# End of the first cross attention: batch tails, router rows and first expert tiles in another order

## The chip, the cores and the metric

The kernel runs on one core of one Trainium2 chip. The metric is the time of one execution on the device in microseconds, as the median of several runs.

## The reference

The input is `x` of 32 batches x 128 tokens x 128 channels, with a context of 32 x 77 x 128. Four blocks follow one another, each added to its input:

```python
x = x + cross_attention_0(context, layernorm(x))   # 16 heads of 64 for q, 4 for k and v, rmsnorm of q and k
x = x + experts(layernorm(x))                      # router over 8 experts, the best 2 of each token
x = x + cross_attention_1(layernorm(x), context)   # 16 heads of 8
x = x + ffn(...)                                   # 2 layers of local attention and a gated feed forward
```

The two blocks that matter here are the first attention and the experts:

```python
attn = softmax(q @ k.T); out = (attn @ v).reshape(B, S_q, H * D) @ wo.T
router_logits = layernorm(x) @ wg.T                 # the two largest of 8, their softmax shares
y = (silu(x @ w1[e].T) * (x @ w3[e].T)) @ w2[e].T    # for the experts e chosen by the token
```

## The kernel before

One program per engine is written out by hand, and the engines meet at semaphores only: TensorE (PE), VectorE (DVE), ScalarE (ACT), GpSimd (POOL) and the DMA queue of SyncE (SP). Each engine executes its own list strictly in the order written.

**First attention.** It is a software pipeline over the 32 batches. In step i the body works on batch i-1 (projections), on i-2 (scores, exponentials), on i-3 (the probabilities `a_p` are turned by 16 transposes, L547, in two halves; ACT, L667, and DVE, L870, copy the halves to `a_pT`; then come the products with the values, L591, and their copy to `a_oT`, L686), on i-4 (output projection, L623, and the addition to `X`, L924, with mean and variance, L933 to L988, and the root on POOL, L993), and on i-5 (a router row: normed by DVE, L718, transposed, L497, copied, L841, multiplied by the gate, L503, and the two largest of 8 found, L848 and L851). After every fourth router row the group of four gets its places in the experts' regions, and POOL scatters the rows to HBM with indirect DMAs (L1009). The router's transpose and the output projection write the same 128 columns of the PSUM tile `R[0]`, so the one has to wait until the other has been read.

**Experts.** The work is 80 tiles of up to 128 routed rows, 40 for each half of the batches (`SEG` = 2). Step i of the tiles transposes the input of tile i (L1102, after which ACT and DVE split it into a high and a low part, L1152 and L1175), does the three products of tile i-1 with w1 and w3 (L459 to L461), the two transposes of tile i-2 (L1125) and the products of tile i-3 with w2 (L1137). ACT makes the silu of tile i-1 (L1157), which needs another table of functions than the exponentials. DVE multiplies with it (L1183) and copies the result (L1190). The tiles of the first half need the rows of the first 16 batches only, so their inputs wait in SBUF long before the attention ends. The tiles of the second half need the rows of all batches.

**Where the two meet.** The attention's pipeline is unrolled up to its step 34, and then the first `HEAD` = 16 steps of the tiles are written out, with what is left of the attention put between them. Conditions on i do that on each engine, on PE for instance:

```python
            for i in range(HEAD):
                step(SEG * NT, 8, tiles, i)
                if i == 0:
                    step(NB, 8, body, NB + 3)
                if i == 2:
                    router(It(NB + 4, (NB + 4) % 8, NB, 8, 1))
```

Step 34 of the attention does, on PE, the transposes of batch 31, the router row of batch 29, the values of batch 31 and the output projection of batch 30. Between tile steps 0 and 1 stands step 35 with the router row of batch 30 and the output projection of batch 31. The router row of batch 31 follows between tile steps 2 and 5. The places of the last group (`group_placed`), the count per expert (`totals`), the tables of the second half (`tables`, `tables_rest`), the positions (`answers`) and the shares of the two experts come between later tile steps.

## Time and profile before

| | us |
|---|---|
| median of 3 runs | 1665.03 |
| lowest and highest of them | 1663.01, 1668.54 |
| the profiled execution | 1662.99 |
| its span | 1661.2 |

| engine | busy, us | share of the span |
|---|---|---|
| PE | 1483.0 | 89% |
| DVE | 1257.8 | 76% |
| ACT | 1112.5 | 67% |
| POOL | 892.5 | 54% |

The profiled execution took 1662.99 us, of which 1661.2 lie between its first and its last instruction. Times below are counted from the start of this span. The granted clock of PE is given as a share of its full 2.4 GHz, so that 0.50 is the lower level of 1.2 GHz. A product in f32 can show as two matmuls, which is why 8 products of the program are x16 in some rows. Matmuls are pipelined, so the end of one and the start of the next overlap.

### The profile page before, as it was taken

The page shows a single profiled execution, that of the slowest core. Times are in us where ns is not written, and L with a number is a line of the kernel's source. Part 1 is how long each engine was busy: PE and PEld are TensorE (multiplying, and loading weights), DVE is VectorE, ACT ScalarE, POOL GpSimd, SP SyncE. Part 2 cuts the span into 40 slices and gives each one's busy share as a digit, 9 for nine tenths or more (in the row PEclk, how much of TensorE's full clock was granted, in tenths as well). Part 3 has the DMA queues.
Part 4 walks back from the last instruction along what each step waited for, and adds up shares of the span by engine and source line. Part 5 has one row for each costly group of instructions (what it writes and reads, how often), then busy time and mean ns, then how long its engine had stood idle before and what let it go on. Part 6 is the DMA issues. An engine that isn't in the chain of part 4 may idle for free.

```text
span 1661.2 us, 38597 instructions
## 1 busy us (share of the span) xinstructions
PE 1483.0 (89%) x12380; PEld 1229.9 (74%) x12443; DVE 1257.8 (76%) x3064; ACT 1112.5 (67%) x2630; POOL 892.5 (54%) x789
## 2 busy tenths in 40 slices
PE   4888888888878998999986999999888999999888
PEld 3777777677766886777765888888776788888766
DVE  6888888888846557898874788888565677777766
ACT  4877777677735556888773777777532777777632
POOL 5667777677723104555424677777402777777600
PEclk9999999999979998999997999999899999999999
DMA  9700000000012322100000000000000000000000
GB/s 384 304 1 9 9 10 11 8 17 11 10 33 82 87 76 65 36 18 20 16 9 7 15 14 15 13 15 14 8 9 4 9 16 13 15 13 15 9 18 38
DMA packets 75554, 61.30 MB, mean 37 GB/s; under 512 B 40256, under 2 KB 61120, under 8 KB 74688
## 3 DMA queue, kind: packets, MB, share of 16 engines
q1 hardware_dynamic: 71360, 51.69, 9.6%
q0 software_dynamic: 4096, 8.40, 1.7%
q8 instruction: 50, 0.82, 0.2%
q14 instruction: 48, 0.39, 0.1%
HBM read 21.30 MB, written 30.41 MB: 31 GB/s over the span
## 4 chain that ended last, share of the span: by engine, by line
DVE 43%; PE 25%; ACT 18%; issue 9%; POOL 3%; DVEq 1%; DMA 1%; SPq 0%; ACTq 0%; POOLq 0%
ACT d_p L708 10%; DVE slot L1713 5%; DVE d_ss L1696 5%; DVE d_B L1704 4%; DVE d_A L1702 4%; PE slot L459 4%; ACT d_sq L1633 4%; PE slot L460 3%; PE slot L461 3%; PE slot L1832 3%; PE slot L547 3%; DVE c_nm L1377 2%; PE slot L1137 2%; DVE a_mx L728 2%; PE slot L623 2%
## 5 line engine op out<-in xcount | busy, mean ns | idle before, releaser
L1750 POOL TENSOR_TENSOR d_r<-d_vv,nhalf 128x16 f32<-128x16 f32 x64 | 186.1, 2907 | 210.6 <-DVE d_vv L1701 210.6
L993 POOL TENSOR_TENSOR rs<-mv,nhalf 128x1 f32 (+1 forms) x160 | 97.9, 612 | 255.0 <-DVE mv L988 190.1
L708 ACT ACTIVATE d_p<-slot,d_nm,d_r 128x128 f32<-128x128 f32 x512 | 185.6, 468 | 49.3 <-DVE d_nm L1717 49.3
L708 ACT ACTIVATE a_p<-slot,a_nm,a_rq 128x77 f32<-128x77 f32 x512 | 163.8, 429 | 36.0 <-DVE a_nm L732 36.0
L1696 DVE TENSOR_REDUCE d_ss<-d_sq 128x16 f32<-128x1024 f32 x64 | 78.1, 1220 | 99.0 <-ACT d_sq L1633 99.0
L1752 POOL TENSOR_TENSOR d_A<-d_A,d_B 128x1024 f32<-128x1024 f32 x64 | 151.3, 2364 | 0.0
L708 ACT ACTIVATE c_p<-slot,c_nm 128x77 f32<-128x77 f32 x512 | 117.4, 361 | 8.6 <-DVE c_nm L1377 8.3
L1617 PE MATMUL slot<-d_v,d_pT 128*128 128x65 f32 x1024 | 121.4, 272 | 0.0
L1617 PEld LDWEIGHTS slot<-d_v,d_pT 128*128 128x128 f32 x1024 | 119.6, 192 | 0.0
L1347 ACT ACTIVATE c_pT<-slot 77x1024 f32<-77x1024 f32 x64 | 67.0, 1047 | 40.5 <-PE slot L1271 40.4
L1048 POOL TENSOR_TENSOR a_rq<-a_vvq,nhalf 128x16 f32<-128x16 f32 x32 | 93.4, 2918 | 0.0
L1713 DVE TENSOR_REDUCE slot<-slot 128x8 f32<-128x1024 f32 x64 | 78.9, 1232 | 12.6 <-PE slot L1590 9.5
L1633 ACT ACTIVATE d_sq<-slot 128x1024 f32<-128x1024 f32 x64 | 67.8, 1059 | 24.8 <-PE slot L461 24.8
L1475 POOL DMA_INDIRECT c_yg<-answers,c_gi x64 | 64.0, 1001 | 36.7 <-POOL c_gi L1471 26.3
L1590 PEld LDWEIGHTS slot<-d_qT 64*128 64x128 f32 x1024 | 62.7, 189 | 27.5 <-issue 27.5
L1704 DVE TENSOR_TENSOR d_B<-slot,T 128x512 f32<-128x512 f32 x128 | 81.8, 681 | 0.0
L1860 ACT ACTIVATE f_gl<-slot,b1l 128x512 f32<-128x512 f32 (+1 forms) x48 | 32.8, 684 | 72.6 <-PE slot L461 72.6
L1271 PE MATMUL slot<-ident,c_p 128*77 128x128 f32 x512 | 71.0, 284 | 11.2 <-ACT c_pT L1347 10.5
L1637 ACT ACTIVATE d_qT<-slot 128x1024 f32<-128x1024 f32 x64 | 65.7, 1027 | 20.3 <-PE slot L1563 20.3
L1009 POOL DMA_INDIRECT routed<-r_xn,r_ps x64 | 64.8, 1013 | 25.0 <-issue 15.9
L1611 PE MATMUL slot<-wol,d_oT 128*128 128x128 f32 x512 | 74.0, 288 | 4.6 <-ACT d_oT L1650 4.6
L1702 DVE TENSOR_TENSOR d_A<-slot,T 128x1024 f32<-128x1024 f32 x64 | 77.9, 1218 | 0.0
(283 smaller groups left out, 4546.2 us busy)
## 6 DMA issues: line engine op xcount, KB each, us to landing
routed<-zero SPq DMA_DIRECT2D x2, 9216.0 KB, 48.9
b_x<-routed SPq DMA_DIRECT2D x80, 64.0 KB, 1.8
answers<-b_y SPq DMA_DIRECT2D x40, 128.0 KB, 1.9
X<-in_x SPq DMA_DIRECT2D x2, 1024.0 KB, 7.3
d_zx<-Z SPq DMA_DIRECT2D x64, 32.0 KB
H<-Z SPq DMA_DIRECT2D x64, 32.0 KB
out<-f_o SPq DMA_DIRECT2D x8, 256.0 KB, 2.0
d_zx<-Z SPq DMA_DIRECT2D x64, 31.8 KB
```

Source lines behind the costliest of these rows:

```text
L708: i = e.activation(t["p"][:, h, :], R[slot][:, k // nbank, nk * (k % nbank):nk * (k % nbank) + nk], ACT.Exp, bias=t["nm"][:, h:h + 1], sca ...
L993: return e.tensor_tensor(rs[:, bass.ds(b, 1)], mv[:, bass.ds(b, 1), 1:2].rearrange("p a b -> p (a b)"), nhalf[:, 0:1], ALU.pow)
L1048: e.tensor_tensor(a["rq"][:, it.m(1, 2), :], a["vvq"][:], nhalf[:, 0:16], ALU.pow).then_inc(S("a_rq"), 1)
L1611: mm = e.matmul(R[1][:, 0, 0:128], t["oT"][:, c, :], wol[:, l, c, :], start=(c == 0), stop=(c == 3))
L1617: mm = e.matmul(R[3][:, h // 4, 65 * (h % 4):65 * (h % 4) + 65], t["pT"][:, 4 * (h % 2) + h // 2, :], t["v1"][:, it.m(4, 4), h, :], start= ...
L1633: e.activation(t["sq"][:].rearrange("p (a b) -> p a b", a=2), qk_slot(it)[:], ACT.Square).then_inc(S("d_sq"), 1)
L1696: e.tensor_reduce(t["ss"][:, p, :], t["sq"][:].rearrange("p (h d) -> p h d", d=DL), AX.X, ALU.add)\
L1702: e.tensor_tensor(A, qk, T1[:, l, :, :].unsqueeze(2).to_broadcast([128, 2, HL, DL]), ALU.mult)
L1704: i = e.tensor_tensor(Bt[:, :, :, 32 * h:32 * h + 32], qk[:, :, :, 32 - 32 * h:64 - 32 * h], T2[:, l, :, 32 * h:32 * h + 32].unsqueeze(2). ...
L1713: e.tensor_reduce(R[0][:, 0, 0:8], R[2][:].rearrange("p a (j k) -> p a j k", k=128), AX.X, ALU.max, negate=True)\
L1750: e.tensor_tensor(t["r"][:, p, :], t["vv"][:, p, :], nhalf[:, 0:16], ALU.pow).then_inc(S("d_key"), 1)
L1752: e.tensor_tensor(t["A"][:, p, :], t["A"][:, p, :], t["B"][:, p, :], ALU.add).then_inc(S("d_key"), 1)
```

## The change

The work and the data are the same. The order on PE, ACT and DVE at the end of the attention is another, and one small activation is added. The pieces of the body become functions (`turned`, `values`, `output`, `second_half`, `added`, `measured`), the common pipeline ends one step earlier (`last_step=NB + 2`), and step 34 is written out piece by piece:

- PE: tile step 0 goes first, then the first half of the transposes of batch 31, the output projection of batch 30, the second half, and the values of batch 31. The output projection of batch 31 follows tile step 1, which holds the first products of tile 0. `output(..., False)` leaves out the wait for a router row, since none stands ahead of it any more.
- The router rows of batches 29, 30 and 31 come after tile steps 2 and 3, 4 and 5, 6 and 7. Places and count move back by two steps (PE 7 to 9 and 9 to 11, DVE 8 to 10), the tables from 10 and 11 to 12 and 13, the positions from 12 and 13 to 14 and 15, the shares behind the last step, and the exponential of the shares on ACT from step 9 to 10.
- ACT: a silu of two elements is put ahead of the wait for the values of batch 31, so that the silu's table is loaded there.

```diff
+            def turned(it, half):
+                b, slot = it.b(3), (2, 3)[half]
+                if half == 0:
...
+                e.wait_ge(S(("ac_na", "ac_nb")[half]), count(b))
+                for c in range(8):
+                    h = 8 * half + 4 * (c // 4) + 2 * (c % 2) + c // 2 % 2
+                    mm = e.transpose(R[slot][0:SK, c // 4, 128 * (c % 4):128 * (c % 4) + 128], a["p"][:, h, :], ident[:])
+                mm.then_inc(S(("ac_PTa", "ac_PTb")[half]), 1)
+
+            def values(it):
+                b = it.b(3)
...
+            def output(it, routed=True):
+                b = it.b(4)
...
+                    if routed and it.b(5) is not None:
+                        e.wait_ge(S("r_v"), count(it.b(5), 4, 4))
+                    if routed and it.b(6) is not None and it.m(6, GB) == 3:
+                        e.wait_ge(S("r_ps"), count(it.b(6)))
+                    e.wait_ge(S("ac_oTe"), count(b))
+                    for c in range(8):
+                        mm = e.matmul(R[0][:, 0, 0:128], a["oT"][:, it.m(4, 2), c, :], wo0[:, c, :], start=(c == 0), stop=(c == 7))
+                    mm.then_inc(S("ac_wo"), 1)
...
-            pipeline(e, NB, 8, 8, body, [A_PART], totals, last_step=NB + 3)
+            pipeline(e, NB, 8, 8, body, [A_PART], totals, last_step=NB + 2)
 
             tiles = b_tensor(e)
-            for i in range(HEAD):
+            tail = [It(NB + i, (NB + i) % 8, NB, 8, 1) for i in range(6)]
+            step(SEG * NT, 8, tiles, 0)
+            turned(tail[2], 0)
+            output(tail[2], False)
+            turned(tail[2], 1)
+            values(tail[2])
+            for i in range(1, HEAD):
                 step(SEG * NT, 8, tiles, i)
-                if i == 0:
-                    step(NB, 8, body, NB + 3)
-                if i == 2:
-                    router(It(NB + 4, (NB + 4) % 8, NB, 8, 1))
-                if i == 4:
-                    logits(It(NB + 4, (NB + 4) % 8, NB, 8, 1))
-                if i == 7:
-                    router(It(NB + 5, (NB + 5) % 8, NB, 8, 1))
+                if i == 1:
+                    output(tail[3], False)
+                if i in (2, 4, 6):
+                    e.wait_ge(S("ac_add"), NB)
+                    if i > 2:
+                        e.wait_ge(S("r_v"), count(NB - 5 + i // 2, 4, 4))
+                    router(tail[1 + i // 2])
+                if i in (3, 5, 7):
+                    logits(tail[1 + i // 2])
                 if i == 9:
+                    router(tail[5])
+                if i == 11:
                     totals(1)
             e.wait_ge(S("r_nr"), SEG)
             return tiles
...
                     e.wait_ge(S("a_nma"), count(b))
                     exponentials(e, a, 2, 0, 4, SK, S("ac_expa"), a["rq"][:, it.m(2, 2), :])
+                if it.static and it.i == NB + 2:
+                    e.activation(g_["s"][:, 0, 0:2], eps[:, 0, :], ACT.Silu)
...
-            pipeline(e, NB, 8, 4, body, [A_PART], last_step=NB + 3)
+            pipeline(e, NB, 8, 4, body, [A_PART], last_step=NB + 2)
 
             tiles = b_scalar(e)
-            for i in range(HEAD):
+            step(SEG * NT, 4, tiles, 0)
+            step(NB, 4, body, NB + 2)
+            for i in range(1, HEAD):
                 step(SEG * NT, 4, tiles, i)
-                if i == 9:
+                if i == 10:
                     e.wait_ge(S("r_dl"), NB)
                     e.activation(r_["dn"][:], r_["dl"][:], ACT.Exp).then_inc(S("r_ex"), 1)
             return tiles
...
+            def added(it):
+                b = it.b(4)
+                if b is not None:
+                    e.wait_ge(S("ac_wo"), count(b))
+                    e.tensor_tensor(rows(X, b), rows(X, b), R[0][:, 0:1, 0:128], ALU.add).then_inc(S("ac_add"), 1)
...
-            pipeline(e, NB, 16, 8, body, [A_PART], both_tables, last_step=NB + 3)
+            pipeline(e, NB, 16, 8, body, [A_PART], both_tables, last_step=NB + 2)
 
             tiles = b_vector(e)
-            for i in range(HEAD):
+            tail = [It(NB + i, (NB + i) % 8, NB, 8, 1) for i in range(6)]
+            step(SEG * NT, 4, tiles, 0)
+            added(tail[2])
+            second_half(tail[2])
+            measured(tail[2])
+            row_normed(tail[2])
+            for i in range(1, HEAD):
                 step(SEG * NT, 4, tiles, i)
-                if i == 0:
-                    step(NB, 8, body, NB + 3)
                 if i == 1:
-                    row_normed(It(NB + 4, (NB + 4) % 8, NB, 8, 1))
-                if i == 3:
-                    row_turned(It(NB + 4, (NB + 4) % 8, NB, 8, 1))
-                if i == 5:
-                    row_chosen(It(NB + 4, (NB + 4) % 8, NB, 8, 1))
-                if i == 6:
-                    group_chosen(It(NB + 4, (NB + 4) % 8, NB, 8, 1))
-                if i == 8:
-                    group_placed(It(NB + 5, (NB + 5) % 8, NB, 8, 1))
+                    added(tail[3])
+                    measured(tail[3])
+                if i in (2, 4, 6):
+                    row_turned(tail[1 + i // 2])
+                if i in (3, 5, 7):
+                    row_chosen(tail[1 + i // 2])
+                    if i < 7:
+                        row_normed(tail[2 + i // 2])
+                if i == 7:
+                    group_chosen(tail[4])
                 if i == 10:
+                    group_placed(tail[5])
+                if i == 12:
                     tables(1)
-                if i == 11:
+                if i == 13:
                     tables_rest(1)
-                if 12 <= i < 12 + SEG:
-                    answers(i - 12)
-                if i == 14:
-                    shares()
+                if i >= 14:
+                    answers(i - 14)
+            shares()
             return tiles
```

The order of PE from the last transposes of the attention to the first products of tile 0 (`wo_127` is the output weight wo0, `a_p` the probabilities, `r_xn` a router row, `b_x` a tile's input, `w13h` the expert weights). Before:

```order
L547 MATMUL slot<-ident,a_p 77x128 x16
L497 MATMUL slot<-ident,r_xn 128x128
L503 MATMUL slot<-wg,r_xT 128x8
L591 MATMUL slot<-a_pT,a_vt 64x256 x8
L623 MATMUL slot<-wo_127,a_oT 128x128 x8
L1102 MATMUL slot<-ident,b_x 128x128
L497 MATMUL slot<-ident,r_xn 128x128
L503 MATMUL slot<-wg,r_xT 128x8
L623 MATMUL slot<-wo_127,a_oT 128x128 x8
L1102 MATMUL slot<-ident,b_x 128x128
L1107 TENSOR_LOAD t_expert
L459 ISA
```

The same stretch of PE in the changed kernel:

```order
L1141 MATMUL slot<-ident,b_x 128x128
L516 MATMUL slot<-ident,a_p 77x128 x8
L554 MATMUL slot<-wo_127,a_oT 128x128 x8
L516 MATMUL slot<-ident,a_p 77x128 x8
L534 MATMUL slot<-a_pT,a_vt 64x256 x8
L1141 MATMUL slot<-ident,b_x 128x128
L1146 TENSOR_LOAD t_expert
L459 ISA
L459 MATMUL slot<-w13h,b_xTl 128x512
L460 REGISTER_ALU
L460 MATMUL slot<-w13l,b_xTh 128x512
L461 MATMUL slot<-w13h,b_xTh 128x512
```

Two router rows (L497, L503) have gone from the stretch, one output projection stands between the two halves of the transposes, and the other one follows the products of tile 0.

On DVE, between tile steps 2 and 5, the changed kernel has this (`r_xT`, `r_mx`, `r_ix` and `r_xn` belong to router rows, the `b_` names to tiles):

```order
L864 COPY r_xT<-slot 128x128
L1214 TENSOR_TENSOR b_xTl<-slot,b_xTh 128x128
L1222 TENSOR_TENSOR b_g<-slot,b_s 128x256
L1229 COPY b_y<-slot 128x128
L871 MAX r_mx<-slot 128x8
L874 MAX_INDEX r_ix<-r_mx,slot 128x8
L741 TENSOR_SCALAR r_xn<-X,mv,rs 128x128
L1214 TENSOR_TENSOR b_xTl<-slot,b_xTh 128x128
L1222 TENSOR_TENSOR b_g<-slot,b_s 128x256
L1229 COPY b_y<-slot 128x128
L864 COPY r_xT<-slot 128x128
```

Before, only the row of batch 31 was spread over the tiles. Now the four small operations of a row come three times, once in every two steps.

## Rows read from the trace of the kernel before

**Rows 1.** The profile page, its first line.

```profile
span 1661.2 us, 38597 instructions
```

**Rows 2.** Waits from 462 to 487 us: total, times, longest.

```profile
ACT a_oT L686 <- PE slot L591: 8.5, 1, 8.5
```

**Rows 3.** Stretches: length; busy PE, PEld, DVE, ACT, POOL (instructions); clock; DMA; GB/s.

```profile
462.00:466.00 4.00, 1.54 (x13) 1.15 (x11) 2.41 (x7) 3.04 (x8) 1.21 (x1) 1.00 0.00 0
466.00:477.00 11.00, 8.90 (x41) 6.37 (x42) 2.64 (x9) 1.02 (x1) 2.63 (x3) 0.53 0.03 12
...
480.00:487.00 7.00, 5.47 (x22) 5.05 (x23) 1.24 (x7) 0.41 (x2) 1.71 (x2) 0.51 0.05 19
487.00:505.00 18.00, 17.19 (x107) 12.91 (x106) 10.12 (x45) 12.24 (x31) 6.43 (x8) 1.00 0.27 79
505.00:518.00 13.00, 9.02 (x49) 6.63 (x49) 12.12 (x43) 5.15 (x18) 11.47 (x10) 1.00 0.29 88
...
530.00:620.00 90.00, 88.03 (x551) 72.41 (x550) 49.05 (x164) 51.69 (x165) 4.26 (x6) 1.00 0.29 82
```

**Rows 4.** Order of time, PE: start, us, engine, line, operation, [idle before <-releaser].

```profile
458.55 1.95 PE L591 MATMUL slot<-a_pT,a_vt 77*64 77x256 f32 x16
460.43 2.05 PE L623 MATMUL slot<-wo,a_oT 128*128 128x128 f32 x16
463.71 1.07 PE L547 MATMUL slot<-ident,a_p 128*77 128x128 f32 x8 [1.24 <-POOL a_p L715]
466.06 1.57 PE L547 MATMUL slot<-ident,a_p 128*77 128x128 f32 x8 [1.28 <-DVE a_p L715]
470.65 3.68 PE L591 MATMUL slot<-a_pT,a_vt 77*64 77x256 f32 x16
474.26 3.21 PE L623 MATMUL slot<-wo,a_oT 128*128 128x128 f32 x16
482.57 3.75 PE L623 MATMUL slot<-wo,a_oT 128*128 128x128 f32 x16 [0.96 <-DVE r_ix L851]
487.87 0.33 PE L1102 MATMUL slot<-ident,b_x 128*128 128x128 f32 x1 [0.39 <-DVE b_xTl L1175]
488.17 0.49 PE L459 MATMUL slot<-w13h,b_xTl 128*128 x1
488.73 0.40 PE L461 MATMUL slot<-w13h,b_xTh 128*128 x1
```

**Rows 5.** Order of time, DVE and ACT, at the end of the attention.

```profile
465.12 0.80 DVE L715 TENSOR_TENSOR a_p<-a_p,a_rc 128x616 f32<-128x616 f32 x1
467.67 1.22 DVE L870 COPY a_pT<-slot 77x1024 f32<-77x1024 f32 x1 [1.02 <-PE slot L547]
474.38 1.02 ACT L686 ACTIVATE a_oT<-slot 128x1024 f32<-128x1024 f32 x1 [8.54 <-PE slot L591]
486.87 1.28 ACT L1157 ACT_TABLE_LOAD   x1
488.16 0.39 ACT L1157 ACTIVATE b_s<-slot 128x256 f32<-128x256 f32 x1
```

**Rows 6.** Order of time, the router row of batch 31 between the tiles.

```profile
488.92 0.34 DVE L718 TENSOR_SCALAR r_xn<-X,mv,rs 128x128 f32<-128x128 f32 x1
489.40 0.30 PE L497 MATMUL slot<-ident,r_xn 128*128 128x128 f32 x1
491.89 0.28 DVE L841 COPY r_xT<-slot 128x128 f32<-128x128 f32 x1
492.81 0.29 PE L503 MATMUL slot<-wg,r_xT 128*128 128x8 f32 x2
495.47 0.16 DVE L848 MAX8 r_mx<-slot 128x8 f32<-128x8 f32 x1
495.86 0.17 DVE L851 FIND_INDEX8 r_ix<-r_mx,slot 128x8 uint32<-128x8 f32 x1
```

**Rows 7.** Order of time, PE: the input of tile 12, behind the tables.

```profile
508.17 0.33 PE L1102 MATMUL slot<-ident,b_x 128*128 128x128 f32 x1 [1.36 <-DVE b_xTl L1175]
```

More of the change, by code:

```diff
@@ new lines, in values @@
+            def values(it):
+                b = it.b(3)
+                if b is not None:
+                    if it.seen(1):
+                        e.wait_ge(S("ac_v"), it.upto(1))
+                    if it.static:
+                        if it.seen(2):
+                            e.wait_ge(S("a_qTe"), it.upto(2))
+                        if it.seen(4):
+                            e.wait_ge(S("ac_oTe"), it.upto(4))
+                    e.wait_ge(S("ac_pTa"), count(b))
+                    e.wait_ge(S("ac_pTb"), count(b))
+                    for g in range(HK0):
+                        for odd in range(2):
+                            mm = e.matmul(R[1][64 * odd:64 * odd + 64, g // 2, 256 * (g % 2):256 * (g % 2) + 256],
+                                          a["v"][0:SK, it.m(3, 4), DH0 * g:DH0 * g + DH0],
+                                          a["pT"][0:SK, 4 * g + 2 * odd:4 * g + 2 * odd + 2, :].rearrange("p a b -> p (a b)"),
+                                          start=True, stop=True)
+                    mm.then_inc(S("ac_PV"), 1)
@@ L536, in body @@
                 if b is not None:
-                    for half, slot in ((0, 2), (1, 3)):
-                        if half == 0:
-                            if it.seen(3):
-                                e.wait_ge(S("ac_expa"), it.upto(3))
-                        else:
-                            if it.seen(3):
-                                e.wait_ge(S("ac_expb"), it.upto(3))
-                        e.wait_ge(S(("ac_na", "ac_nb")[half]), count(b))
-                        for c in range(8):
-                            h = 8 * half + 4 * (c // 4) + 2 * (c % 2) + c // 2 % 2
-                            mm = e.transpose(R[slot][0:SK, c // 4, 128 * (c % 4):128 * (c % 4) + 128], a["p"][:, h, :], ident[:])
-                        mm.then_inc(S(("ac_PTa", "ac_PTb")[half]), 1)
+                    for half in range(2):
+                        turned(it, half)
                 b = it.b(1)
@@ L609, in body @@
                     mm.then_inc(S("a_pj"), 1)
-                b = it.b(4)
-                if b is not None:
-                    if it.seen(1):
-                        e.wait_ge(S("a_ev"), nth(it.upto(1), 3, 3))
-                    if it.static:
-                        if it.seen(5):
-                            e.wait_ge(S("ac_add"), it.upto(5))
-                    if it.b(5) is not None:
-                        e.wait_ge(S("r_v"), count(it.b(5), 4, 4))
-                    if it.b(6) is not None and it.m(6, GB) == 3:
-                        e.wait_ge(S("r_ps"), count(it.b(6)))
-                    e.wait_ge(S("ac_oTe"), count(b))
-                    for c in range(8):
-                        mm = e.matmul(R[0][:, 0, 0:128], a["oT"][:, it.m(4, 2), c, :], wo0[:, c, :], start=(c == 0), stop=(c == 7))
-                    mm.then_inc(S("ac_wo"), 1)
+                output(it)
                 if it.static and it.i == 3:
@@ L871, in body, with measured @@
                         .then_inc(S("ac_pTb"), 1)
+            def added(it):
+                b = it.b(4)
+                if b is not None:
+                    e.wait_ge(S("ac_wo"), count(b))
+                    e.tensor_tensor(rows(X, b), rows(X, b), R[0][:, 0:1, 0:128], ALU.add).then_inc(S("ac_add"), 1)
+            def measured(it):
+                b = it.b(4)
+                if b is not None:
+                    e.wait_ge(S("ac_add"), count(b))
+                    apart(e)
+                    e.bn_stats(st[:, 0, :], rows(X, b)).then_inc(S("ac_bn"), 1)
+                    stats_tail(e, b, S("ac_bn"), S("ac_ag"), S("ac_ve"))
+            def body(it):
+                b = it.b(0)
+                if b is not None:
+                    layernorm(e, X, a["xn"], b, it.m(0, 2)).then_inc(S("ac_xn"), 1)
+                second_half(it)
                 row_normed(it)
@@ L920, in body @@
                     i.then_inc(S("a_kTe"), 1)
[L921 to L924 removed]
+                added(it)
                 b = it.b(2)
@@ L929, in body @@
                     normalize(e, a, slice(8, 16), SK).then_inc(S("ac_nb"), 1)
[L930 to L934 removed]
+                measured(it)
                 if it.static and it.i < NB // ST:
```

44 lines of the change are left out of this document (13 added, 31 removed).

## The prediction

> **What bounds the kernel now.** The page comes first: the span is 1661.2 us [rows 1], and the profiled execution took 1662.99. The change touches only the seam between the first attention and the expert tiles, so the second view is the waits from 462 to 487 us. The longest stands at ACT: 8.5 us in one piece until PE has made the values of batch 31 [rows 2]. The third view is the stretches. The reader is to see that no engine is full in the seam. From 462 to 466 us PE is busy for 1.54 of 4 us, and from 466 to 477 DVE is busy for 2.64, ACT for 1.02 and POOL for 2.63 of 11 us; PE shows 8.90, but at a granted clock of 0.53 [rows 3]. The batches left are one chain of transposes, copies, values, projection, addition, root and router row, and PE executes it in written order. From 487 us on the tiles fill PE, 17.19 of 18 us and later 88.03 of 90 at clock 1.00 [rows 3]. So the seam is a latency, and behind it a stage starts in which PE sets the pace. Whatever brings the first tiles forward brings all 80 tiles and what follows forward by as much, unless something else is late then.
>
> The last view is the order of time. It fixes two marks. The program is unchanged up to the output projection of batch 29, which ends at 460.43 + 2.05 = 462.48. The second mark is the transpose of tile 2's input, at 487.87 [rows 4]. In both programs it stands behind the last output projection and the first products of tile 0. Between the marks lie 25.39 us.
>
> **The change part by part.** I walk the new order of PE between these marks, with durations at full clock where a row has one.
>
> 1. Tile 0's transpose, about 0.3, falls into the gap ahead of the transposes of batch 31. These start at 463.71, because POOL's normalization releases them [rows 4], and nothing of that moves: to 463.71.
> 2. The first half of the transposes is 1.07 [rows 4]: 464.78.
> 3. The output projection of batch 30, 2.05 as at 460.43 [rows 4]: 466.83. Its input was copied a step earlier, and its wait for the router is dropped. It delays the second half of the transposes, which is ready when DVE's normalization ends, 465.12 + 0.80 = 465.92 [rows 5], by 0.9.
> 4. The second half, 1.07 like the first: 467.90.
> 5. DVE copies it, 1.22 [rows 5], plus 0.05 for the handover: 469.17. The addition of batch 30 stands ahead on DVE and is over by about 467.2.
> 6. The values of batch 31, 1.95 as those of batch 30 at 458.55 [rows 4]: 471.12. The router row of batch 29 no longer stands here.
> 7. ACT's copy, 1.02 [rows 5], plus 0.05: 472.19. Tile 1's transpose lies beside it.
> 8. The products of tile 0. They write a bank that this copy reads, so they start behind it. From 488.17 to the last one's start at 488.73 and on to its issue's end are some 0.8 us [rows 4]: 472.99.
> 9. The output projection of batch 31, 2.05: 475.04. Then tile 2's transpose, at about 475.1.
>
> That is 487.87 - 475.1 = **12.8 us** sooner, if PE's clock is full.
>
> **Clock.** The rows show 1.00 up to 466 us, then 0.53 until 477 and 0.51 from 480 to 487 [rows 3]. It fell after a stretch in which PE was busy for 1.54 of 4 us. In the new order the same stretch holds about 3 of 4 us, and the gaps that are left are some 0.9, 1.3 and 1.0 us. So it may stay up, but the values and projections come in bursts. At the lower level (1.2 GHz) the values took 3.68 in place of 1.95, and a projection 3.21 or 3.75 in place of 2.05 [rows 4], 1.2 to 1.7 more for each such burst. The bounds are none of them and three, 0 to 4.9. I take one, **-1.5**, since the new seam is fuller than the one in which the clock fell, and less full than the tiles.
>
> The Trainium skill says on the page "TensorE: Matmul & The Clock Gate", section "What's actually happening", that the throttled state is the default and that activity releases it. The trace agrees in that the clock came back while the projection of batch 31 ran.
>
> **Router rows.** Two more rows, of batches 29 and 30, now stand between tiles on a full PE. Each has a transpose of 0.30 and a gate product of 0.29 [rows 6], which makes 2 x 0.59 = **-1.2**. On DVE a row costs 0.34 for the norm, 0.28 for the copy, and from 495.47 to 496.03 for the largest two [rows 6], 1.2 in all. From 487 to 505 DVE was busy for 10.12 of 18 us [rows 3], so two rows more, 2.4 us, fit into the free time of some eight tiles. I cost them at nothing, with up to 1.5 if DVE comes late with a tile's low part.
>
> **Silu's table.** Its load, 1.28, now lies in ACT's wait for the values, where 8.5 us were free and some 5 remain. Before, it stood ahead of the first silu, which started right behind it at 488.16 [rows 5]. PE was on tile 1's products until 488.73 + 0.23 and lost little by it. I take 0, and 0.6 as the upper bound.
>
> On the page "ScalarE: Activation LUTs", section "What ACT_TABLE_LOAD costs", the Trainium skill puts a switch at 1283 ns of load and 1380 ns of drain. The load of 1.28 agrees and no such drain is seen ahead of 488.16; with it the sum would be some 1.4 us better.
>
> **Late things.** Places, tables and positions are the same work with the same stall: tile 12's input waited 1.36 for DVE behind the tables [rows 7], and PE was busy for 9.02 of 13 us there [rows 3]. They move back by two tile steps, that is some 3.5 us, against 10 gained, so they too come earlier in time. The inputs of the second half's tiles need them from tile 40 on. That is 24 tiles behind the written-out ones. The 551 matmuls in 90 us [rows 3], at 10 for a tile, make 1.64 us for each, 39 us together, so neither SP's loads nor POOL's scatters delay it. POOL's three instructions of 2.63 us from 466 to 477 [rows 3] are a root and the two scatters that stand between the roots of batches 30 and 31. They fit between the two additions, which by the steps above lie 8 us apart.
>
> **Sum.** 12.8 - 1.5 - 1.2 = **10.1 us** gained. Against the profiled execution's own time that is 1662.99 - 10.1 = 1652.9. The median of the runs is 2.0 higher, at 1665.03, and would give 1654.9. The lowest run equals the profiled one. I put the forecast in the middle, at **1654.0**, from a base of 1664.0.
>
> **The rivals.**
>
> *Lost between the tiles.* A router row now passes from PE to DVE and back in every two steps, and POOL or DVE may be late with it: PE's transpose of a row waits for the previous row's largest two, for the norm and for the last addition. If each of the six pieces stopped PE for about 1 us, less than the 1.36 of [rows 7], 6 of the 10 us would go, and the time would be 1660, no change that can be told. Against it: between 487 and 505 us PE was busy for 17.19 of 18 us although one such row passed through there [rows 3]. Chance 0.08.
>
> *The change does less than it says.* The second half of the transposes waits for the projection of batch 30. If the three bursts of the clock's upper bound ran at the lower level, the gain would be 12.8 - 4.9 - 1.2 = 6.7 and the time 1657.3. That is inside the forecast's range.
>
> *Slower: the clock through the tiles.* The rows of the router cut the tiles' stream on PE, and if PE is granted the lower level through the 14 written-out steps that follow, each tile of 1.64 us takes about 1.3 longer, by the ratio of 3.75 to 2.05 of the projection [rows 4]. This is 18 us against 10, and the time is 1672. It decides if the clock falls again behind 476 us and doesn't come back before the places are made; two tiles at that level would not be enough. Against it: from 505 to 518 us PE was busy for only 9.02 of 13 and kept 1.00 [rows 3]. Chance 0.04.
>
> **How the numbers follow.** The forecast with its clock variants has 0.88. A measurement of this kernel can tell about 0.3%, or 5.0 us, from no change. The gain's own bounds are 12.8 + 0.6 - 0 = 13.4 and, with three bursts at the lower level, DVE's 1.5 and the rows' 1.2, 12.8 - 4.9 - 1.5 - 1.2 = 5.2. From 1664.0 that gives 1650.6 to 1658.8. The runs shown spread by 5.5 us, so I put one us on the lower and half a one on the upper end: 1649.5 to 1659.3. The rivals on the far side, at 1660 and 1672, stay out, with 0.12. Faster by over 0.3% is 0.88, within it 0.08, slower by over 0.3% 0.04.
>
> **What the new profile would show.** Tile 0's first products should start near 472, not 486, and tile 2's transpose near 475 to 477. ACT's wait for the values should shrink from 8.5 to 4 or 5 us with a table load inside it. The clock between 466 and 480 should be well above 0.53. The tiles should fill PE from about 476 on, with no idle time over 0.5 us at L497 or L503, and the shift of 10 us should still be there at tile 40 and at the last tile. I am wrong if the shift is there at tile 2 and has gone by the last tile, or if the second half of the transposes or the copy behind it waits for something that I have not named.

## The result, and the profile after

| | before | after |
|---|---|---|
| median of the runs of the comparison, us | 1666.09 (20 runs) | 1659.62 (20 runs) |
| lowest, highest | 1661.67, 1681.12 | 1652.89, 1668.67 |
| profiled execution, its span | 1662.99, 1661.2 | 1662.73, 1660.9 |

The ratio is 0.9961, 95% interval 0.9947 to 0.9976: 6.5 us or 0.39% faster, where 10.1 us were forecast. The profiled executions differ by 0.26 us only, because the part behind the tiles took 1046.1 us in that of after and 1040.3 in that of before (more on this part below). The page shows about the same busy times as before:

```profile
span 1660.9 us, 38661 instructions
...
PE 1488.3 (90%) x12442; PEld 1232.7 (74%) x12443; DVE 1258.8 (76%) x3064; ACT 1112.3 (67%) x2631; POOL 892.2 (54%) x789
```

Waits of the changed kernel from 462 to 487 us (total, times, longest), to be read against [rows 2]:

```profile
ACT a_oT L707 <- PE slot L534: 3.5, 1, 3.5
```

The 8.5 us of ACT have become 3.5. The stretches of the changed kernel (columns as in [rows 3]):

```profile
462.00:466.00 4.00, 2.87 (x27) 2.66 (x26) 2.44 (x6) 3.35 (x10) 1.21 (x1) 1.00 0.06 16
466.00:477.00 11.00, 8.68 (x51) 7.33 (x50) 3.79 (x12) 2.84 (x5) 5.15 (x6) 0.72 0.09 31
480.00:487.00 7.00, 6.41 (x44) 5.37 (x44) 4.91 (x22) 3.57 (x12) 3.13 (x4) 1.00 0.33 97
487.00:505.00 18.00, 14.03 (x92) 10.61 (x90) 11.70 (x52) 9.81 (x26) 6.35 (x7) 1.00 0.28 82
505.00:518.00 13.00, 9.52 (x50) 7.78 (x51) 9.25 (x27) 4.57 (x15) 7.42 (x6) 0.87 0.17 51
530.00:620.00 90.00, 86.32 (x540) 71.02 (x540) 50.21 (x171) 50.46 (x161) 4.97 (x8) 1.00 0.27 78
```

From 480 to 487 us PE is now at full clock on tiles, where it stood at 0.51 before [rows 3]. Two stretches fall short. From 466 to 477 the clock is 0.72, better than 0.53 but not full. And from 505 to 518, where the positions and the shares now stand together, it is 0.87, where it was 1.00. The seam in order of time, PE and one row of ACT, against [rows 4, 5]:

```profile
464.55 1.95 PE L554 MATMUL slot<-wo,a_oT 128*128 128x128 f32 x16
465.78 1.28 ACT L703 ACT_TABLE_LOAD   x1
468.77 1.95 PE L534 MATMUL slot<-a_pT,a_vt 77*64 77x256 f32 x16 [1.41 <-DVE a_pT L890]
471.93 0.79 PE L459 MATMUL slot<-w13h,b_xTl 128*128 x1 [0.92 <-ACT a_oT L707]
473.37 3.62 PE L554 MATMUL slot<-wo,a_oT 128*128 128x128 f32 x16
476.77 0.42 PE L1141 MATMUL slot<-ident,b_x 128*128 128x128 f32 x1
```

The projection of batch 30 and the values take 1.95, full clock. Behind the pause of 0.92 the first product takes 0.79, where [rows 4] has 0.49, and the last projection 3.62: one burst at the lower level. Tile 2 is turned at 476.77, where it was 487.87. That is 11.1 us sooner. The shift is 10.3 at tile 17 (519.22 before, 508.93 after). At tile 18 it is 6.0 (521.01, 514.98), and it stays at 6.1 up to tile 79 (620.89, 614.78). So more than four us go in a single step, between tiles 17 and 18. All engines there, in the changed kernel:

```profile
506.71 2.25 POOL L1490 MEMSET c_vz<- 128x2560 f32 x1
508.11 0.42 DVE L836 TENSOR_TENSOR h_eq<-h_eq,h_dx 128x256 f32<-128x256 f32 x1
508.56 0.42 DVE L839 TENSOR_REDUCE h_sh<-h_eq 128x32 f32<-128x256 f32 x1
508.88 1.84 POOL L1491 MEMSET d_v<- 128x2080 f32 x1
508.93 0.27 PE L1141 MATMUL slot<-ident,b_x 128*128 128x128 f32 x1
509.13 1.86 DVE L982 TENSOR_SCALAR r_w<-r_dn 128x32 f32<-128x32 f32 x1
511.02 0.35 DVE L984 RECIPROCAL r_w<-r_w 128x32 f32<-128x32 f32 x1
511.41 0.19 DVE L986 TENSOR_TENSOR r_w<-r_dn,r_w 128x32 f32<-128x32 f32 x1
511.82 0.29 DVE L1214 TENSOR_TENSOR b_xTl<-slot,b_xTh 128x128 fp32r<-128x128 f32 x1 [0.21 <-DVE r_w L986]
512.26 0.79 PE L459 MATMUL slot<-w13h,b_xTl 128*128 x1 [3.06 <-DVE b_xTl L1214]
514.98 0.39 PE L1141 MATMUL slot<-ident,b_x 128*128 128x128 f32 x1
```

DVE does the last positions (to L841, not all shown) and the three operations of the shares (L982 to L986) in one go. The first share operation, 128 x 32 elements, shows 1.86 us, and ends 0.27 after POOL's memset of `d_v` (508.88 + 1.84 = 510.72, and 509.13 + 1.86 = 510.99). The low part of the next tile comes behind all that. PE waits 3.06 us for it, and resumes at the lower clock. In the kernel before, the same operation met only the memset's last part:

```profile
514.58 1.85 POOL L1452 MEMSET d_v<- 128x2080 f32 x1
516.07 0.61 DVE L949 TENSOR_SCALAR r_w<-r_dn 128x32 f32<-128x32 f32 x1
```

### The profile page after: what moved, and what is told of

It is laid out like the page before. It is cut to its first block, busy times and chain, and to the rows that moved or that the text cites. A ratio compares the mean times of both kernels' runs of the same rounds, so it can differ in the third digit from the quotient of the medians.

```text
span 1660.9 us, 38661 instructions
## 1 busy us (share of the span) xinstructions
PE 1488.3 (90%) x12442; PEld 1232.7 (74%) x12443; DVE 1258.8 (76%) x3064; ACT 1112.3 (67%) x2631; POOL 892.2 (54%) x789
## 4 chain that ended last, share of the span: by engine, by line
DVE 43%; PE 25%; ACT 18%; issue 9%; POOL 3%; DVEq 1%; DMA 1%; SPq 0%; ACTq 0%; POOLq 0%
ACT d_p L731 10%; DVE slot L1752 5%; DVE d_ss L1735 5%; DVE d_B L1743 4%; DVE d_A L1741 4%; PE slot L459 4%; ACT d_sq L1672 4%; PE slot L460 3%; PE slot L461 3%; PE slot L1871 3%; PE slot L516 3%; DVE c_nm L1416 2%; PE slot L1176 2%; DVE a_mx L751 2%; DVE c_rcT L1469 1%
## 5 line engine op out<-in xcount | busy, mean ns | idle before, releaser
L613 PE MATMUL slot<-a_kb,a_qT 128*128 128x154 f32 x512 | 77.5, 294 | 0.7 <-ACT a_pT L686 0.4
```

The source lines that it names most:

```text
L613: mm = e.matmul(R[slot][:, k // 2, 2 * SK * (k % 2):2 * SK * (k % 2) + 2 * SK], a["qT"][:, c, :], a["kb"][:, it.m(2, 2), c // 2, :], start ...
```

## The experiments

Theories at the start: (A) the memset on POOL holds the share operation; (B) the lump of positions and shares on DVE is too long by itself; (C) the clock fall in the seam is the loss. The early silu was a fourth suspect.

**How the runs are read.** The runs come in three groups, each on a chip of its own; the tables number them. Medians did not separate the variants: the 95% intervals of the ratios are 0.3% to 0.7% wide, 5 to 11 us. Behind the tiles, from tile 79's transpose to the end of the span, executions took 1040 to 1052 us in the first pair and on the chips of groups 2 and 3, without an order by kernel, and 1071 to 1080 in group 1, whose chip is slower. So the traces are compared up to tile 79, from a mark before anything changed: the start of the addition of batch 29 on DVE. The table gives the start of a tile's transpose (L1102 or L1141) less this mark, and the duration of the one DVE operation in dispute. The run b_before is the kernel before unchanged, c_after and c_after_again are the changed kernel unchanged. Each row is one trace.

| group, kernel | tile 2 | 10 | 17 | 18 | 20 | 40 | 79 | first share |
|---|---|---|---|---|---|---|---|---|
| before | 25.36 | 39.35 | 56.71 | 58.50 | 61.47 | 94.44 | 158.38 | 0.61 |
| after | 14.33 | 30.15 | 46.49 | 52.54 | 55.59 | 88.41 | 152.34 | 1.86 |
| 1 c_after | 14.44 | 31.52 | 56.18 | 58.24 | 61.18 | 94.06 | 157.98 | 0.17 |
| 1 e1 | 12.10 | 29.11 | 50.49 | 52.81 | 55.76 | 88.59 | 152.51 | 0.17 |
| 1 e2 | 12.12 | 29.20 | 52.77 | 55.00 | 57.95 | 90.82 | 154.82 | 0.17 |
| 1 e3 | 12.12 | 29.20 | 52.81 | 55.98 | 58.92 | 91.76 | 155.72 | 0.17 |
| 2 b_before | 23.94 | 37.85 | 55.21 | 57.00 | 59.97 | 92.91 | 156.88 | 0.62 |
| 2 b8 | 23.94 | 37.81 | 54.87 | 56.87 | 59.84 | 92.77 | 156.69 | 0.17 |
| 2 e7 | 12.06 | 27.89 | 44.78 | 46.97 | 49.92 | 82.75 | 146.74 | 0.17 |
| 2 e4 | 12.07 | 27.75 | 44.10 | 50.11 | 53.43 | 86.33 | 150.37 | 1.86 |
| 3 c_after_again | 12.07 | 27.87 | 44.65 | 49.84 | 53.59 | 86.46 | 150.40 | 1.47 |
| 3 e1_again | 12.07 | 27.88 | 44.62 | 47.70 | 50.65 | 83.49 | 147.42 | 0.17 |
| 3 e2_again | 12.07 | 27.84 | 44.15 | 46.35 | 49.30 | 82.12 | 146.05 | 0.17 |
| 3 e9_all | 12.07 | 27.64 | 43.97 | 46.16 | 49.26 | 82.16 | 146.04 | 0.17 |

| run | median, us | the kernel before beside it | ratio, 95% interval |
|---|---|---|---|
| c_after | 1699.13 | 1702.19 | 0.9968 [0.9950, 0.9987] |
| e1 | 1693.96 | same | 0.9958 [0.9941, 0.9975] |
| e2 | 1696.12 | same | 0.9968 [0.9950, 0.9986] |
| e3 | 1696.12 | same | 0.9962 [0.9948, 0.9976] |
| b_before (1 execution) | 1673.58 | 1671.06 | none |
| b8 | 1668.47 | same | 0.9991 [0.9962, 1.0021] |
| e7 | 1654.87 | same | 0.9914 [0.9881, 0.9947] |
| e4 | 1656.82 | same | 0.9908 [0.9880, 0.9935] |
| c_after_again | 1657.72 | 1668.23 | 0.9925 [0.9895, 0.9955] |
| e1_again | 1655.88 | same | 0.9928 [0.9903, 0.9953] |
| e2_again | 1657.96 | same | 0.9932 [0.9905, 0.9958] |
| e9_all | 1656.43 | same | 0.9912 [0.9884, 0.9940] |

**The changed kernel again, group 1.**

> The changed kernel once more, as it is, to see whether what its first trace shows repeats. Two theories. A (a stall at the seam's end): the first trace has a shift of 10.3 us against the kernel before up to tile 17's input, and 6.0 from tile 18 on to tile 79, since DVE makes the positions of the second half and the shares in one piece, and the shares' first operation takes 1.86 us beside a memset of POOL. A expects the shift again at 10.3 at tile 17 and at 6 from tile 18 on, DVE's first share operation at 1.8 to 1.9 us, PE idle for about 3 us ahead of the next products, and a time 6 us below that of the kernel before (ratio 0.996). B (given back later, at random): the 6 us of the times come out of the later stages, so the shift at tile 79 may be 10 in this trace.

The signs that A named did not repeat: the first share took 0.17 and the stall between tiles 17 and 18 was gone (2.06 us). B is not decided, since group 1 has no trace of the kernel before and so shows no shift. Yet nothing was gained by the missing stall, as another operation was held, for longer:

```profile
507.43 0.95 POOL L1048 DMA_INDIRECT routed<-r_xn,r_ps  x1 [0.30 <-issue]
507.69 4.96 DVE L822 TENSOR_SCALAR t_read<-h_ba 128x40 int32<-128x40 f32 x1
508.37 2.26 POOL L1490 MEMSET c_vz<- 128x2560 f32 x1
510.55 1.86 POOL L1491 MEMSET d_v<- 128x2080 f32 x1
512.72 0.17 DVE L825 SCALAR_TENSOR_TENSOR h_dx<-h_dx,region 128x8 f32<-128x8 f32 x1
```

A conversion of 128 x 40 elements, 0.18 us in the first trace, lasts until 512.65, 0.24 behind the end of both memsets (512.41). The memsets meet whatever DVE happens to be at, here the tables.

**e1: the memsets behind the shares.**

```diff
             e.wait_ge(S("ac_add"), count(NB - 1))
+            e.wait_ge(S("r_w"), 11)
             e.memset(c_["vz"][:], 0.0).then_inc(S("c_const"), 1)
```

> POOL's four memsets wait for the shares, so that nothing of POOL runs beside them. If the memset holds the first share operation up (A1), it falls from 1.86 to 0.2 to 0.6 us, the idle time of PE ahead of the products of tile 16 from 3.1 to about 1.8, and the shift at tile 79 grows from 6 to 7.3 or more, up to 8.5 if PE's clock no longer falls there. If the operation is slow by itself or the size of the lump on DVE is all that counts (A2), nothing changes: 1.86 and a shift of 6.

Neither operation is held. The conversion stands in the same place as in c_after, some 0.27 after the start of POOL's last indirect DMA (505.16 here), and only the memset behind that DMA is gone:

```profile
505.43 0.18 DVE L822 TENSOR_SCALAR t_read<-h_ba 128x40 int32<-128x40 f32 x1
...
513.23 2.23 POOL L1491 MEMSET c_vz<- 128x2560 f32 x1 [7.10 <-DVE r_w L986]
```

Tile 79 is 5.5 us sooner than in c_after (152.51 against 157.98), of which 2.3 are already there at tile 2: c_after had the seam's clock fall and e1 had not. That leaves 3.1 for the memsets on this chip. The median is 5.2 lower, and doesn't decide by itself. With nothing held, e1 still isn't free of a stall: from tile 2 to tile 17 it takes 38.39 us, where the same program takes 32.55 in e1_again, and its clock from 505 to 518 is 0.74 (0.65 in c_after). This loss belongs to group 1 and isn't explained (see the slower chip, at the end).

**e2: the shares in time for step 11**, with a semaphore `r_sh` of their own.

```diff
+                if i == 11:
+                    shares()
...
-            shares()
...
-            e.wait_ge(S("r_w"), 11)
+            e.wait_ge(S("r_sh"), 3)
```

> The shares are made behind tile step 11, away from the positions and from the memsets. If the lump of positions and shares together with the memset costs the 4.3 us (A), PE's wait of 3 us ahead of tile 16's products is gone or under 1 us, the shift at tile 79 is 9 to 10, and the time is 9 to 10 us below that of the kernel before, ratio 0.994. If only the memset counts, it is 7.5 to 8.5. If the change's gain is lost in later stages (B), the time does not move against the changed kernel whatever the shift.

The first share took 0.17, but the memset held the tables, 4.97:

```profile
504.56 4.97 DVE L822 TENSOR_SCALAR t_read<-h_ba 128x40 int32<-128x40 f32 x1
505.25 2.25 POOL L1491 MEMSET c_vz<- 128x2560 f32 x1
```

So moving the shares alone protects the shares alone.

**e3: no early silu.** The activation of two elements is left out; it has no part in the result.

```diff
-                if it.static and it.i == NB + 2:
-                    e.activation(g_["s"][:, 0, 0:2], eps[:, 0, :], ACT.Silu)
```

> The silu of two elements is left out, so that the table is loaded ahead of the first real silu. The first forecast put its worth at 0, 0.6 at most: PE is on the output projection of batch 31 for over 2 us (3.6 in the first trace) while ACT loads for 1.28 us, so the shift at tile 2 and the time stay within 0.3 us and 0.1%. If a switch costs 2.7 us with a drain, as the Trainium skill has it on the page ScalarE: Activation LUTs, it is still below 3.6, but the first silu would start 2.7 instead of 1.3 us behind the end of tile 0's products.

```profile
472.77 1.28 ACT L1194 ACT_TABLE_LOAD   x1
474.06 0.38 ACT L1194 ACTIVATE b_s<-slot 128x256 f32<-128x256 f32 x1
```

Tile 2 stands at 12.12, as with the silu (12.10 and 12.12). Tile 79 stands 2.3 ahead of c_after, which is c_after's clock fall. The early table is worth nothing that a trace shows.

**The kernel before, and it with late memsets.** b8 has e1's wait in the program before.

> The kernel before once more, for a trace from the same chip as the runs beside it. In the runs so far an operation of DVE on data in SBUF took far longer than its work where POOL's memsets ran (1.86 in place of 0.17 us for the first share, 4.96 in place of 0.18 for the row addresses of the second half's tiles, L822). If that is a matter of where the two meet in time, this kernel shows which of its operations meet a memset here: the theory A1 expects that any such operation of one input that starts within the memsets' 6 us ends only when they do, and that those outside take 0.2 us.

> The kernel before with POOL's four memsets behind the shares. A1 (memsets hold DVE up): tables and shares take 0.2 us each per operation, and the time falls by the stall that b_before's trace shows, 0.5 to 5 us. It is also the fair partner of the changed kernel with late memsets: if the change in order itself is worth 10 us as forecast, that kernel stays some 8 to 10 us below this one (ratio 0.994 to 0.995). If the order is worth only what the times showed, 5 to 6 us, the distance is that.

The first share goes from 0.62 to 0.17, tile 79 from 156.88 to 156.69, and the ratio has 1 inside. The kernel before had nothing to lose there:

```profile
513.68 1.85 POOL L1452 MEMSET d_v<- 128x2080 f32 x1
515.17 0.62 DVE L949 TENSOR_SCALAR r_w<-r_dn 128x32 f32<-128x32 f32 x1
```

The expected 0.5 to 5 us did not come. The held operation is thus a cost that came with the change of order. The theory in the expectation of b_before was also too wide: TENSOR_REDUCE, which has one input too, started inside the memset of `c_vz` at 511.56 and again inside that of `d_v` at 513.88, and took 0.42 both times, as it does alone.

**e7: both.** e2, and the memsets behind the positions (`r_w` at 8).

> The changed kernel with both: the memsets wait for the positions, and the shares are made behind tile step 11. A1 alone expects what late memsets alone gave, 10.3 to 11 us at tile 17 and at tile 79 against the kernel before on this chip with no memset in the way. A2 (the lump of positions and shares costs time of its own) expects 1 to 1.5 us more than late memsets alone.

```profile
507.51 0.19 DVE L841 SCALAR_TENSOR_TENSOR r_pos<-h_sh,r_pr 128x32 uint32<-128x32 f32 x1
507.83 2.23 POOL L1492 MEMSET c_vz<- 128x2560 f32 x1 [3.27 <-DVE r_pos L841]
508.14 0.49 PE L459 MATMUL slot<-w13h,b_xTl 128*128 x1 [0.45 <-DVE b_xTl L1215]
```

PE waits 0.45 at the place where it waited 3.06, and its product takes 0.49. Tile 17 to 18 is 2.2 us. Tile 79 is 10.1 us ahead of b_before: the shift survives. That is just short of the 10.3 to 11 expected. In this trace the clock was at its lower level from 497 to 501 us, between tiles 13 and 14, which goes with a tile 17 that is 0.6 to 0.8 later than in e9_all and e2_again (below).

**e4: PE kept busy in the seam.** Transposes of the identity, whose results nobody reads, stand in the two pauses.

```diff
+            def busy(slot, n):
+                for c in range(n):
+                    e.transpose(R[slot][:, 0, 128 * (c % 4):128 * (c % 4) + 128], ident[:], ident[:])
...
             turned(tail[2], 1)
+            busy(1, 10)
             values(tail[2])
+            busy(2, 7)
```

> Ten transposes of the identity into a free bank while PE waits for the second copy of the probabilities, and seven while it waits for the copy of the values' products; nobody reads them. In two of five traces of the changed order the projection of batch 31 took 3.62 us at the lower clock, in the other three 1.95. If PE's idle gaps bring the clock down there, it is 1.95 now and the clock 1.00 from 462 to 480 us, worth 2.2 us in those executions and about 1 us in the median. If the fall has another cause, it stays, and the extra products may add up to 0.5 us where they end later than the copy they bridge. The stall behind the tables stays as it is.

Tile 2 stands at 12.07, like the unfilled kernels without a fall. They are at full clock as well: e7, in the same group and not filled, has 12.06. So the fill costs nothing, and since the clock fell in only 2 of the 9 unfilled traces of this seam (after and c_after), two filled ones without a fall prove nothing. The run is inconclusive on the fill. On the other point it is clear: with the seam at full clock, tile 17 to 18 still takes 6.0 us and the first share 1.86. (C) is not the main loss.

**Group 3, one chip: the changed kernel, e1, e2 and everything.** e9_all is e7 with e4's fill.

> The changed kernel as partner of the three beside it, since the chips differ. By the traces so far the tiles lose 3.6 to 4.3 us between the inputs of tiles 17 and 18 (6.0 us in place of 1.8 to 2.2) if the first share starts inside a memset, as in the first trace; if the row addresses start inside one, as in c_after, they lose more and the share nothing. One of the two is expected, and 1 to 3 us in the seam by PE's clock.

> Memsets behind the shares, on another chip. Seen from the addition of batch 29, tile 79's input comes at 146.7 us with late memsets and early shares and at 150.4 to 152.3 with the stall. A1 (the memset alone): r_w takes 0.17 us, PE does not wait 3 us, its clock stays up, and tile 79 is at 147 to 147.5. A2 (the lump of positions and shares counts for itself): 148 to 149, with a wait of PE of 1.3 to 2 us ahead of the products of tile 16.

> Shares behind tile step 11, memsets where they were. If no row address meets a memset (they start about 0.7 us later than in the changed kernel, and the memsets came 1.5 to 2.4 us behind them in two traces), tile 79 is at 146.7 to 147.5 as with both changes; if one does, as on the slower chip, it stops for up to 5 us and tile 79 is at 151 or later. Either way the first share takes 0.2 us.

> Late memsets, early shares and the filled gaps together. PE's clock stays at 1.00 through the seam in every execution and no operation of DVE meets a memset: tile 2's input at 12.1, tile 79's at 146.7, and a median 1 us below that of late memsets with early shares, since the seam's clock fell in some executions only; 9 to 11 us below the kernel before by the trace, with a ratio of 0.991 to 0.994.

The four seams are equal at tile 2 (12.07). The share beside the memset, and then PE, in c_after_again:

```profile
507.87 1.84 POOL L1491 MEMSET d_v<- 128x2080 f32 x1
508.51 1.47 DVE L982 TENSOR_SCALAR r_w<-r_dn 128x32 f32<-128x32 f32 x1
511.25 0.49 PE L459 MATMUL slot<-w13h,b_xTl 128*128 x1 [2.67 <-DVE b_xTl L1214]
```

and in e1_again:

```profile
505.31 0.17 DVE L982 TENSOR_SCALAR r_w<-r_dn 128x32 f32<-128x32 f32 x1
506.22 2.23 POOL L1491 MEMSET c_vz<- 128x2560 f32 x1 [3.74 <-DVE r_w L986]
506.75 0.49 PE L459 MATMUL slot<-w13h,b_xTl 128*128 x1 [1.36 <-DVE b_xTl L1214]
```

The same stretch of 20 us (columns as in [rows 3]) in c_after_again:

```profile
500.00:520.00 20.00, 15.34 (x81) 12.48 (x80) 14.66 (x47) 7.81 (x24) 10.51 (x9) 0.88 0.24 70
```

in e1_again:

```profile
500.00:520.00 20.00, 16.84 (x104) 13.43 (x102) 13.36 (x49) 9.64 (x32) 7.91 (x6) 1.00 0.26 76
```

and in e2_again:

```profile
500.00:520.00 20.00, 17.52 (x104) 14.02 (x105) 14.28 (x52) 9.67 (x31) 9.89 (x8) 1.00 0.30 86
```

The clock goes from 0.88 to 1.00 and PE executes 104 matmuls in place of 81. Tile 79 stands at 150.40, then 147.42 with late memsets, then 146.05 with early shares. The memset cost 3.0 us (A): 2.1 of it lie between tiles 17 and 18 (5.19 against 3.08), and 0.8 between tiles 18 and 20, where the clock had fallen behind PE's wait (3.75 against 2.95).

Tile 79 of e1_again is where A1 put it (147 to 147.5), with the wait that A2 named. Of the 1.4 between e1_again and e2_again the lump (B) explains 0.9: tile 17 to 18 takes 3.08 with it and 2.20 without, and the wait of 1.36 left in e1_again is 0.45 in e7. The other 0.5 is there at tile 17 already. It goes with a fall of the clock around tile 13, in e1_again:

```profile
492.00:502.00 10.00, 7.98 (x33) 5.85 (x34) 7.30 (x28) 4.84 (x13) 7.26 (x8) 0.83 0.30 91
```

and in e2_again no such fall:

```profile
492.00:502.00 10.00, 7.91 (x45) 5.64 (x44) 7.54 (x31) 6.49 (x17) 5.47 (x6) 1.00 0.30 89
```

c_after_again and e7 had it too (0.83 in the same stretch), after, e4 and e9_all had not (1.00), so it goes neither with the shares nor with the memsets. The 3.0 of A is free of it, as both traces had it; the 0.9 of B rests on one pair. In group 1 the lump doesn't show: e1 takes 2.32 from tile 17 to 18 and e2 2.23, but e1 at the lower clock.

e2_again kept its memsets early and had nothing held in this trace, but on the chip of group 1 the same program lost 4.97 in the tables. e9_all gets 146.04 with the memsets out of the way as well.

The medians of these four runs lie within 2.1 us of each other and their intervals overlap, so a version that beats the change is not shown by the times. By the traces e7 (of group 2), e2_again and e9_all reach tile 79 some 3.7 to 4.4 us sooner than c_after_again. The ratios don't follow: the lowest, 0.9908, is that of e4, which still has the stall.

## Why the prediction was right in part

**The bottleneck and the seam: right.** Tile 2's transpose was forecast near 475.1 at full clock, 476.6 with one slow burst; it came at 476.77 with one slow burst. The projection of batch 30 was to start at 464.78 (464.55), the values at 469.17 (468.77), ACT's copy to end at 472.19 (the products followed at 471.93). The gain at full clock, 12.8 by the steps, is 25.36 - 12.07 = 13.3 against the first trace of before and 23.94 - 12.07 = 11.9 against b_before, whose own clock fell later.

**The clock: right for one execution, no property of the kernel.** "One burst, -1.5" was 2.3 where it occurred (14.33 - 12.07), since the products of tile 0 run slowly too. But 7 of 9 traces of this seam have no fall. One reading of the old rows was wrong: the clock had not come back while the projection of batch 31 ran. That one was slow to its end (3.75, to 486.32, clock 0.50 from 485.0 to 486.3). It came back during the projection of batch 30, which the 3.21 at 474.26 shows. And the bound of 4.9 for three slow bursts isn't the sum of its rows, 1.73 + 1.16 + 1.70 = 4.6. Neither changes the forecast.

**Router rows: right.** Forecast 1.2. From tile 2 to 79 the kernels with nothing held and no lump need 133.98 (e2_again), 133.97 (e9_all) and 134.68 (e7, with the clock's fall at tile 13), against 133.02 and 132.94 before: 1.0, and 1.7 with the fall. The rival that lost six single microseconds on these rows didn't occur, though its time, 1660, is what was measured. No idle time over 0.5 us stands at the router's two lines in the trace of after. It stands at the tiles' own operands, where the tables now come: 0.74, 0.78 and 1.02 ahead of three of them from 498 to 505 us, the stall that the forecast called the same.

**Silu's table: right at 0,** by e3.

**The step that failed** is the one on late things: "Places, tables and positions are the same work with the same stall". The work is the same; its neighbours are not. The sum has nothing for it, and it took 4.3 us. The prediction judged it by one deadline only, the inputs of tile 40, and DVE's extra operations by the free time of a whole stretch. Two things were missed. The shares, moved behind the last written step, now follow the positions of the second half directly, and DVE serves the tiles only when both are done. And POOL's memsets, which it hadn't listed, follow its last scatters and came 5.7 us forward with them (the one of `d_v` from 514.58 to 508.88), while the first share came 6.9 forward (516.07 to 509.13) and so met 1.2 us more of it. Both lie between tiles 17 and 18, 6.05 us in place of 1.79. The sum, mended, in the first pair of traces: seam 11.0, tiles 2 to 17 -0.8 (32.16 against 31.35), tile 17 to 18 -4.3, the rest +0.1, together 6.0. In the later traces it is 156.88 - 150.40 = 6.5: there the seam is 11.9, and what follows takes 5.4 back: 3.0 the memset, 0.9 the lump, 0.5 with the clock's fall at tile 13 and 1.0 the rows. These two traces are from two chips.

**The number.** 1659.62 lies 5.6 us above the forecast of 1654.0 and 0.3 above the end of the range, 1659.3. About 2.1 of the 5.6 are the base: the forecast started from 1664.0, out of three runs, and the 20 runs of the comparison gave 1666.09 for the kernel before. The rest is the gain, 6.5 in place of 10.1. It lies inside the gain's own bounds of 5.2 to 13.4, but by luck: the lower bound was built on three bursts at the lower clock, of which one at most occurred, and its DVE term had an upper bound of 1.5 us where the stall cost 4.3. The nearest row for the stall was there: 12.12 of 13 us DVE busy and 11.47 POOL in the stretch of the tables [rows 3], with 1.36 idle at PE [rows 7]. An upper bound from there, a DVE block of a few operations whole on the path, would have held it.

## What to carry to other kernels

When a seam (the place where one stage hands over to the next) is shortened, go through everything on the same engines up to the next barrier, also the fillers that nobody waits for: if their release moves by another amount than their neighbours, they meet other work. A long memset on GpSimd should be placed where VectorE has no TENSOR_SCALAR from SBUF to SBUF on the path; that is the form which was held here. A block of small VectorE operations that was cheap in two halves, with the tiles served in between, may delay the next tile when it stands in one piece, by 0.9 us here. And where the time's scatter is as large as the effect, compare traces from a mark that the change doesn't touch; it showed differences of 3 and 1 us here, which the medians didn't. Read the clock of each stretch beside it: 0.5 us that looked like the lump's went with a fall of the clock.

## What the runs showed of the hardware

**VectorE held by GpSimd's memset.** `TENSOR_SCALAR` with one f32 input in SBUF and its output in SBUF: 0.17 alone, 0.61, 0.62, 1.47 or 1.86 beside the memset of `d_v`, ending 0.25 to 0.27 behind its end (516.68 against 516.43 before, 509.98 against 509.71 in c_after_again). The same ends lie 0.04 to 0.05 behind the end of the memset that follows, the short one of `d_zx` (510.99 against 510.95 in after), so which of the two ends lets go can't be told. The Trainium skill says, on the page "SBUF — State Buffer", section "SBUF: two separate sides", that the pair of ports that the two engines share is an exclusive lock. These rows agree. `TENSOR_TENSOR` on two SBUF inputs beside the memset of `c_vz` took 0.42, starting at 508.11 while the memset ran to 508.96, and was not held; that agrees as well, since the Trainium skill, in the same section, has such an operation contend only with a GpSimd operation that reads SBUF. One input isn't enough to be held: TENSOR_REDUCE, with one input in SBUF, started at 508.56 beside the same memset and took 0.42, as alone, and RECIPROCAL took 0.35 at 511.02, as alone, beside the memset of one partition that ran from 510.90 to 512.73.

**Held over two memsets.** On the chip of group 1 the 128 x 40 conversion lasted 4.96, 4.97 and 4.98 (c_after, e2, e3). Each time it started some 0.26 us after POOL's last indirect DMA did, 0.7 before the first memset is shown to begin, and was let go only behind the second memset. In e1 it stood there too and took 0.18, with the same DMA beside it and no memset behind. So it is the memsets that hold it, also one that the trace shows as not yet begun, and the change from one to the next frees nothing. By the shown starts, the operation that began first was not the one that went through. Whether the start shown for either engine is the moment at which it takes its ports, the traces can't tell. On the other chips this conversion came earlier against the scatters (504.35 in after, with the last scatter at 505.67), and was not met. The bare order in time of two engines decides here, and it differs from chip to chip.

**The clock in the same program.** Nine unfilled traces of this seam have the same pauses on PE, of 1.4 us and less; in two the clock fell to its lower level for the first products of tile 0 and the last projection, which cost 2.3 us, in seven it didn't. In the seam before, with pauses of 1.24 and 1.28 [rows 4] and up to 2.6 later, it fell in all three traces: the clock is 0.53 from 466 to 477 us in before [rows 3], 0.75 in b_before and 0.77 in b8. Around tile 13 it fell in three of the seven traces of the new order in the first pair and groups 2 and 3, and at tile 17 these three are 0.4 to 0.8 us behind the other four.

**No pause between table load and silu.** Load 1.28, silu 0.01 behind its end, before [rows 5] and in e3.

**A slower chip.** The kernel before took 1702 us in group 1 and 1666 to 1671 elsewhere. In group 1 the waits (total, times, longest) of c_after have entries put down to "remote":

```profile
ACT b_xTh L1191 <- remote: 5.7, 2, 4.0
...
ACT b_s L1196 <- remote: 2.6, 1, 2.6
...
DVE b_y L1229 <- remote: 1.5, 1, 1.5
```

They stand in e1 as well, where nothing was held (ACT 5.8 in two waits, DVE 1.5), and in none of the traces after, b_before, e7 and c_after_again. In e1, ACT starts on tile 15's input at 504.77, though its transpose on PE was over at 501.87. What they are is open. The traces of group 1 also show no landing time for the tile loads and the scatters, which the others do (1.8 and 2.3 us), so a wait that a DMA ended could hardly show there under its own name; whether that is the cause isn't shown.
